# Four graph layers in one kernel: the attention stage's node products at the end of PE's step, and two batches of forward gathers begun behind the scatter

## The chip, the cores and the metric

One NeuronCore of a Trainium2 chip runs the whole program. The metric is the device time of one execution in microseconds, lower is better. The kernel is written directly in instructions for each engine: PE (TensorE, matrix products), DVE (VectorE), ACT (ScalarE), POOL (GpSimd, here the issuer of indirect DMAs) and SP (SyncE, here the issuer of plain DMAs). Engines wait for each other on semaphores only.

## The reference

Four layers run one after the other on a graph of 6250 nodes with 128 features and 106250 edges (two directions of 50000 edges, and a loop on every node), each followed by a residual and a layer norm: `x = layernorm(x + layer(x))`. Edges come sorted by destination. The first layer is attention with 8 heads of 16, and this is what it computes:

```python
q, k, v = (einsum('ni,hid->nhd', x, W) + b for W, b in ((Wq, bq), (Wk, bk), (Wv, bv)))
e = edge_weight[:, None, None] * We[None]
alpha = einsum('ehd,ehd->eh', q[dst], k[src] + e) / sqrt(16)
m = segment_max(alpha, dst)
ex = exp(alpha - m[dst])
w = ex / max(segment_sum(ex, dst)[dst], 1e-16)
agg = segment_sum(w[:, :, None] * (v[src] + e), dst)
out = (agg + skip).reshape(n, 128) @ Wo + bo + x
out = layernorm(out) * gamma + beta
```

The second layer is an edge MLP with a segment sum by destination, the third a filter (`c * (W(edge_attr) * h1[src])`, summed by destination). The fourth is gated: it takes the mean of `x @ W_in` over sources for each destination, and of `x @ W_out` over destinations for each source, and puts both through a GRU cell with `x` as its state.

## The kernel before

The edges lie in 880 tiles of 128 (with fillers, so that no tile crosses more than one bucket of 128 destinations). Four tiles are a batch (U = 4), so each stage runs over BATCHES = 220 batches; the nodes are 49 buckets of 128. For each batch POOL issues four indirect DMAs, one for each tile, which gather the rows of the edges' sources (`gather_rows`, L694) into a ring: six batches deep in the attention stage (KR), seven in the gated one (FR). There are four stages: attention (about 190 to 1415 us), edge MLP (1422 to 2440), filter (2540 to 3650) with a scatter of the rows into an order by source (3650 to 4818, L2221, four indirect DMAs for each batch), and the gated stage (4860 to 6007).

**Attention stage.** Each engine has a loop of its own over slots `s`, and the order of the calls in its body is the order of its work; semaphores tie the loops together. In slot `s` PE multiplies one-hot rows with the queries of batch `s` (`query`, L888), and sums batch `s - 10` into PSUM (`total`, L934: eight products, two of each tile, in two halves; a half waits until DVE has added the half before it to the accumulator, semaphore `added`). DVE multiplies and reduces batch `s - 1` (`products`, `head_sums`), weighs the messages of batch `s - 9` (`weigh`, `message`, L1201) and makes four adds to the accumulator for batch `s - 11` (`add`, L1224), spread over its step. ACT makes the one-hot matrices (`edge_hot`, `turned_hot`) and copies the values out of the gather ring (`keep_values`, L1021), which frees the ring for POOL.

Four batches are a chunk, with its softmax maximum found by scans over the edges. The chunk's work is spread over four phases, `ph = s % 4`, and hops between PE and DVE. In phase 1 PE transposes the scores (`turn_scores`, L896) and DVE scans them in phase 2 (L1157). At the end of phase 2 PE turns the ends of the runs (`turn_runs`, L899 and L900), and DVE walks over them at the start of phase 3 (`walk`, L1169). At the end of phase 3 PE turns the carries (`turn_carries`, L909), ACT copies them in phase 0 (L1039), DVE scans again. At the end of phase 0 PE turns the maximum back (`return_max`, L914, L899, L900), and DVE subtracts it at the start of phase 1 (`shift`, L1188). Before the `total` of each chunk's first batch PE makes `rank_one` (L922, L923). In PE's slot all these transposes stand behind `total`.

**Node parts.** Once all edges of a bucket are added (slot NODE_AT), its 128 nodes go through the rest of the layer in small parts, each in a slot of its own: DVE joins the heads (lag 1), PE turns them (`turn_heads`, lag 2, L944, L945), PE multiplies by Wo (`mix_heads`, lag 3, L949 to L951), DVE's first and second norm (lags 4 and 5) and renewal (lag 6), PE turns the new nodes (`turn_nodes`, lag 7, L955) and projects them for the next layer (`project`, lag 8, L960 to L962). `node_sums(s)` holds PE's parts and `take_nodes(s)` ACT's copies of them out of PSUM (L1063 for the first, L1066, L1068, L1075 and L1076 for the others). DVE's node parts stand last in its slot.

**From the scatter to the gated stage.** A stage's work stands in blocks; all engines meet between two blocks. The filter stage's block ends on POOL with the scatters, then gathers for the first FR = 7 batches of the gated stage into its ring, then a wait for the scatters' landing. In the gated stage's block DVE begins with two memsets of 128 x 6400 elements (L2408, L2409) and then makes the one-hot matrices of the forward part, PE sums batch 0 (`gl_sum_f`, L2376) and so frees the first slot of the ring, for which POOL's next gather waits. SP loads the rows in order by source.

Of the kernel before, what the change touches and what calls it, by code (L numbers as in the profile page):

```python
# [40 lines left out]
KR, FR = 6, 7  # L41
TILES = -(-(E // P + NB) // (U * R)) * U * R
BATCHES = TILES // U
# [726 lines left out]
def node_due(s, lag):  # L770

    return NODE_AT.index(s - lag) if s - lag in NODE_AT else None
# [12 lines left out]
def stage_attention(nc, c, t, small_weights):  # L785


    with ExitStack() as ctx:
# [38 lines left out]
        maxed, returned, shifted, fallen, exped = (sem(n) for n in ("maxed", "returned", "shifted", "fallen", "exped"))  # L827
        ranked, rescaled = sem("ranked"), sem("rescaled")
        hots, exs, ews, messages, summed, added = (sem(n) for n in ("hots", "exs", "ews", "messages", "summed", "added"))
        SLOTS_N = NODE_AT[-1] + PROJECTED + 1  # L830
        PREPARED = 11
        block = ctx.enter_context(nc.Block())

# [7 lines left out]
        @block.sync  # L841
        def _(sp):
            def load_skip(n):
                at = bucket_in_turn(nc, c, n, SP_ENGINE)
                at_least(sp, given, node_groups_before(NODE_AT[n - 2] + TURNED + 1) if n >= 2 else 0, None)
                sp.dma_start(skip[:, n % 2, :], c.skip[bass.ds(at, 1), :, :].rearrange("one p f -> p (one f)")).then_inc(skipped[n % 2], 16)

            def send_rows(n):
                at = bucket_in_turn(nc, c, n, SP_ENGINE)
                sp.wait_ge(taken, node_reads_before(NODE_AT[n] + PROJECTED + 1))  # L850
                sp.dma_start(c.table3[bass.ds(at, 1), :, :].rearrange("one p f -> p (one f)"), rows_out[:, n % 2, :]).then_inc(row_sent[n % 2], 16)

            sp.dma_start(last, c.key[P - 1:P, :]).then_inc(lasts, 16)
            for to, of in small_weights:
                sp.dma_start(to, of).then_inc(weights, 16)
            sp.dma_start(c.table3[NT - 1, :, :], c.x[:, NT - 1, :]).then_inc(padded, 16)
            for k in range(SLOTS_N + 4):
                n = node_due(k, -2)
                if n is not None:
                    load_skip(n)  # L860
                n = node_due(k, PROJECTED + 4)
                if n is not None:
                    send_rows(n)
                if k >= BATCHES:
                    continue
                at_least(sp, hots_t, 2 * (k - R + 1), None)
                load_local_rows(sp, c, rows, k, k % R, rows_in)
                if k % CB == CB - 1:
                    n = k // CB
                    if n == 0:  # L870
                        sp.wait_ge(start, 4)
                    at_least(sp, maxed, 2 * (n - 1), None)
                    breaks = c.breaks[n * CT:(n + 1) * CT, :].unsqueeze(0).broadcast_to([H, CT, P])
                    sp.dma_start(pen[:, n % 2, 0:P], breaks).then_inc(pens_in[n % 2], 16)
            sp.wait_ge(padded, 16)
            for q in range(2):
                sp.wait_ge(row_sent[q], 16 * len(range(q, NB, 2)))

        @block.tensor
        def _(pe):  # L880
# [94 lines left out]

            for s in range(SLOTS_N):
                ph, n = phase(s)
                if s < BATCHES:
                    query(s)
                node_sums(s)  # L980
                km = s - LAG - 1
                if 0 <= km < BATCHES:
                    if km % CB == 0:
                        rank_one(km // CB)
                    total(km)
                if ph == 1 and 0 <= n < CHUNKS:
                    turn_scores(n)
                if ph == 2 and 0 <= n < CHUNKS:
                    turn_runs(n)
                if ph == 3 and 0 <= n < CHUNKS:  # L990
                    turn_carries(n)
                if ph == 0 and 0 <= n - 1 < CHUNKS:
                    return_max(n - 1)

        @block.scalar
        def _(act):
# [81 lines left out]
            for s in range(SLOTS_N):  # L1078
# [2 lines left out]
                    turned_hot(0)  # L1081
                if 0 <= s - LAG - 1 < BATCHES:
                    edge_hot(s - LAG - 1)
                if ph == 0 and 0 <= n - 1 < CHUNKS:
                    carries(n - 1)
                if s + 1 < BATCHES:
                    turned_hot(s + 1)
                for lag, w in ((FIRST, 0), (SECOND, 1)):
                    if node_due(s, lag + 1) is not None:
                        inverse_root(node_due(s, lag + 1), w)  # L1090
                if ph == 1 and 0 <= n - 1 < CHUNKS:
                    exponents(n - 1)
                if 0 <= s - 1 < BATCHES:
                    keep_values(s - 1)
                if 0 <= s - LAG < BATCHES:
                    exps(s - LAG)
                if ph == 1 and 0 <= n < CHUNKS:
                    spreads(n)
                take_nodes(s)

        @block.vector
        def _(dve):
# [202 lines left out]
def stage_edges(nc, c, name, table, acc, buckets, local, layer, h1, ring, arrived, begun, next_rows=None):  # L1305
# [5 lines left out]
    with ExitStack() as ctx:  # L1311
# [60 lines left out]
        def _(pool):  # L1372
            gather_rows(pool, c, table, ring, arrived, [(freed, 1)], range(begun, BATCHES))
            if layer == 2:
                for k in range(BATCHES):
                    c.by_source.scatter(pool, k)
                pool.wait_ge(c.by_source.tabled, 16)
                gather_rows(pool, c, c.table, c.by_source.ring_f, c.by_source.arrived_f, [], range(FR))
                for r in range(R):
                    pool.wait_ge(c.by_source.scattered[r], 16 * U * BATCHES // R)  # L1380
            if layer == 1:
# [590 lines left out]
        stage_attention(nc, c, t, small_weights)  # L1972


E1_R, BEGUN = 6, 3


def stage_src_lists(nc, c, t, loads, before, previous, w_both, b_both, ring, arrived):
# [285 lines left out]
def stage_gated(nc, c, fwd, rev, ring_f, arrived_f, p_in, p_out, gate_rows, out):  # L2264
# [5 lines left out]
    with ExitStack() as ctx:  # L2270
# [16 lines left out]

        @block.gpsimd
        def _(pool):
            gather_rows(pool, c, c.table, ring_f, arrived_f, [(summed_f, 1)], range(FR, BATCHES))  # L2290

        @block.sync
        def _(sp):
# [318 lines left out]
```

## Time and profile before

| | |
|---|---|
| time, median of 3 runs | 6020.16 us (6016.43 to 6023.98) |
| profiled execution, its own time | 6009.66 us |
| its span | 6007.6 us |
| mean granted clock of PE, share of full speed | 0.778 |
| PE busy | 3885.8 us (65% of the span) |
| DVE busy | 3669.8 us (61%) |
| ACT busy | 2801.3 us (47%) |
| POOL busy | 4295.4 us (71%) |
| chain that ended last | POOL 13% of the span, issue 4%, PE 1% |

The shares are means over four stages with different limits, so they say little by themselves. Rows further down come from windows (busy time of each engine in a stretch of the span), from the list of waits (which engine stood at which line, and for whom), and from the timeline (start and length of each instruction in us, and in brackets the idle time before it with what ended it). L934 is line 934 of the kernel. A line may group some instructions of one kind that follow each other: x4 are four of them, and the length is that of all.

### The profile page before, as it was taken

The page shows a single profiled execution, that of the slowest core. Times are in us where ns is not written, and L with a number is a line of the kernel's source. Part 1 is how long each engine was busy: PE and PEld are TensorE (multiplying, and loading weights), DVE is VectorE, ACT ScalarE, POOL GpSimd, SP SyncE. Part 2 cuts the span into 40 slices and gives each one's busy share as a digit, 9 for nine tenths or more (in the row PEclk, how much of TensorE's full clock was granted, in tenths as well). Part 3 has the DMA queues.
Part 4 walks back from the last instruction along what each step waited for, and adds up shares of the span by engine and source line. Part 5 has one row for each costly group of instructions (what it writes and reads, how often), then busy time and mean ns, then how long its engine had stood idle before and what let it go on. Part 6 is the DMA issues. An engine that isn't in the chain of part 4 may idle for free. (4 is left out here: it accounts for less than half of the span.)

```text
span 6007.6 us, 92656 instructions
## 1 busy us (share of the span) xinstructions
PE 3885.8 (65%) x20652; PEld 3141.3 (52%) x20652; DVE 3669.8 (61%) x11763; ACT 2801.3 (47%) x6925; POOL 4295.4 (71%) x4477
## 2 busy tenths in 40 slices
PE   5577777775766776678888887444344346666665
PEld 5466666664555555545655655333333346664443
DVE  6788888886988888666777765111011034445665
ACT  3688888882211111145555654111111158884444
POOL 2677777763777777767777777777777767777775
PEclk8788878887999888878888887555555579898887
DMA  4444444453755555622333325333233245552223
GB/s 125 121 136 131 130 131 129 128 116 101 200 149 145 149 148 148 127 65 74 74 77 74 75 73 100 83 79 78 78 79 78 70 133 168 165 166 79 58 57 45
DMA packets 485359, 652.55 MB, mean 109 GB/s; under 512 B 119512, under 2 KB 332245, under 8 KB 484822
## 3 DMA queue, kind: packets, MB, share of 16 engines
q0 software_dynamic: 155552, 349.05, 23.3%
q1 hardware_dynamic: 329271, 297.58, 18.8%
q8 instruction: 187, 3.06, 0.2%
q14 instruction: 349, 2.86, 0.2%
HBM read 495.44 MB, written 150.71 MB: 108 GB/s over the span
## 5 line engine op out<-in xcount | busy, mean ns | idle before, releaser
L694 POOL DMA_INDIRECT kv_ring<-keys_values,gather_i x880 | 862.2, 980 | 348.9 <-issue 258.4
L694 POOL DMA_INDIRECT arena<-table,gather_i x880 | 856.4, 973 | 291.1 <-issue 266.4
L694 POOL DMA_INDIRECT e_ring<-filter_rows,gather_i x880 | 841.8, 957 | 299.8 <-issue 267.9
L2221 POOL DMA_INDIRECT rows_by_src<-arena,key x880 | 858.3, 975 | 268.7 <-issue 267.6
L694 POOL DMA_INDIRECT e_ring<-table,gather_i x880 | 844.5, 960 | 275.0 <-issue 264.8
L2133 PE MATMUL e_pt<-nodes,arena 128*128 x1728 | 442.5, 437 | 628.5 <-ACT arena L2142 620.9
L2133 PEld LDWEIGHTS e_pt<-nodes,arena 128*128 128x128 f32 x1728 | 381.2, 325 | 690.3 <-issue 690.3
L2125 DVE TENSOR_SCALAR arena<-arena,part 128x512 f32<-128x512 bf16 x220 | 115.2, 525 | 913.1 <-PE e_pt L2133 910.9
L2376 PE MATMUL gl_sum_f<-arena,gl_hot_f 128*128 128x128 f32 x1760 | 282.6, 310 | 446.0 <-DMA arena<-table,gather_i 173.9
L1582 PE MATMUL e_pa<-e_msg,e_hot 128*128 128x128 f32 x3520 | 543.9, 305 | 30.5 <-DVE e_msg L1803 22.7
L743 DVE TENSOR_TENSOR arena<-arena,e_pa 128x128 f32 x1760 | 497.4, 283 | 99.9 <-PE e_pa L1582 70.5
L934 PE MATMUL at_pa<-at_msg,at_hot 128*128 128x145 f32 x1760 | 379.3, 358 | 230.1 <-DVE arena L1224 209.5
L1582 PEld LDWEIGHTS e_pa<-e_msg,e_hot 128*128 128x128 f32 x3520 | 503.4, 220 | 42.9 <-DVE e_msg L1803 34.6
L2376 PEld LDWEIGHTS gl_sum_f<-arena,gl_hot_f 128*128 128x128 f32 x1760 | 243.8, 214 | 485.1 <-DVE gl_hot_f L2416 292.1
L1563 PE MATMUL e_ph<-l_w1e_by_tile,e_attr 128*128 128x512 f32 x440 | 281.5, 726 | 328.5 <-DVE e_tmp L1798 300.7
L2140 ACT ACTIVATE arena<-src_local 128x4 f32<-128x4 bf16 x216 | 45.0, 208 | 932.7 <-DMA rows_by_src<-arena,key 932.5
L934 PEld LDWEIGHTS at_pa<-at_msg,at_hot 128*128 128x128 f32 x1760 | 297.4, 232 | 295.3 <-issue 217.9
L1456 ACT ACTIVATE e_msg<-e_tmp 128x512 f32<-128x512 f32 x220 | 138.6, 630 | 632.8 <-DVE e_tmp L1798 629.2
L1554 PE MATMUL e_pt<-e_attr,L_mlp_w_held 50*128 50x512 f32 x440 | 273.3, 704 | 187.5 <-DVE e_soft L1809 184.8
L2323 ACT ACTIVATE gl_hot_r<-j,arena 128x128 f32<-128x128 f32 x1024 | 324.3, 387 | 150.2 <-PE gl_sum_r L2367 86.9
L888 PE MATMUL at_pq<-arena,at_hot_t 128*128 x1760 | 333.6, 348 | 55.6 <-ACT at_hot_t L1006 44.7
L1565 PEld LDWEIGHTS e_ph<-arena,e_hot_t 128*128 128x128 f32 x1760 | 281.2, 228 | 131.0 <-issue 131.0
(463 smaller groups left out, 9784.5 us busy)
## 6 DMA issues: line engine op xcount, KB each, us to landing
rows_by_src<-e_filler SPq DMA_DIRECT2D x256, 260.0 KB
arena<-rows_by_src SPq DMA_DIRECT2D x256, 260.0 KB, 2.9
at_rows<-local_rows SPq DMA_DIRECT2D x220, 128.0 KB, 3.5
e_rows<-local_rows SPq DMA_DIRECT2D x220, 128.0 KB
arena<-local_rows SPq DMA_DIRECT2D x220, 128.0 KB
e_attr<-edge_attr SPq DMA_DIRECT2D x880, 25.0 KB
kv_ring<-keys_values,gather_i POOLq DMA_INDIRECT x880
e_ring<-table,gather_i POOLq DMA_INDIRECT x880
```

The source lines that it names most:

```text
L694: pool.indirect_dma_start(ring[:, r, u, :], None, table, bass.IndirectOffsetOnAxis(index, 0)).then_inc(arrived[r], 16)
L743: self.dve.tensor_tensor(to, to, self.psum[:, u, 0:self.width], ALU.add).then_inc(self.added, 1)
L888: ins = pe.matmul(pq[:, q, u, 0:QW], hot_t[:, q, u, :], c.query[:, bass.ds(which[u], 1), :].rearrange("p one f -> p (one f)"), start=True, ...
L934: ins = pe.matmul(sum_of(u), hot[:, q, u, :], msg[:, q, u, :], start=True, stop=True)
L1554: pe.matmul(pt[:, r % 2, :, :].rearrange("p u f -> p (u f)"), c.w["mlp_w0"][:, :], attr[:, r, :], start=True, stop=True).then_inc(ready, 1)
L1563: pe.matmul(ph[:, q, :, :].rearrange("p u f -> p (u f)"), attr[:, r, :], c.w["w1e_by_tile"][:, :], start=True, stop=False)
L1565: ins = pe.matmul(ph[:, q, u, :], hot_t[:, r, u, :], c.by_dst[:, bass.ds(which[u], 1), :].rearrange("p one f -> p (one f)"), start=False, ...
L1582: ins = pe.matmul(pa[:, q, u, :], hot[:, r, u, :], msg[:, q, u, :], start=True, stop=True)
L2133: ins = pe.matmul(ph[:, k % 2, u, :], self.hot_t[:, k % R, u, :], self.c.x[:, bass.ds(which[u], 1), :].rearrange("p one f -> p (one f)"), ...
L2221: pool.indirect_dma_start(self.table, bass.IndirectOffsetOnAxis(place, 0), self.out[:, r, u, :], None)\
L2323: act.activation(hot_r[:, r, u, :], c.j[:, 0:P], ACT.Abs, bias=ring_r[:, j % RR, u, F + 1:F + 2], scale=-1.0).then_inc(hots_r, 1)
L2376: ins = pe.matmul(sum_f[:, q, u, :], hot_f[:, r, u, :], ring_f[:, k % FR, u, :], start=True, stop=True)
```

## The change

In the attention stage PE's `node_sums(s)` moves from its place between `query` and `rank_one`/`total` to behind `total`, ahead of the transposes. ACT's `take_nodes` moves from the end of the slot to a place behind `turned_hot` and takes the products of the slot before; `turned_hot` comes ahead of `carries`, and `keep_values` ahead of `exponents`. The stage has one slot more, and SP's sending of node rows stands one slot later. Behind the scatter two batches of forward gathers are begun (BEGUN_F), not seven; the gated stage's block issues the rest.

```diff
-        SLOTS_N = NODE_AT[-1] + PROJECTED + 1
+        SLOTS_N = NODE_AT[-1] + PROJECTED + 2
...
-            for k in range(SLOTS_N + 4):
+            for k in range(SLOTS_N + 5):
...
-                n = node_due(k, PROJECTED + 4)
+                n = node_due(k, PROJECTED + 5)
...
                 if s < BATCHES:
                     query(s)
-                node_sums(s)
                 km = s - LAG - 1
                 if 0 <= km < BATCHES:
                     if km % CB == 0:
                         rank_one(km // CB)
                     total(km)
+                node_sums(s)
                 if ph == 1 and 0 <= n < CHUNKS:
                     turn_scores(n)
...
                     edge_hot(s - LAG - 1)
+                if s + 1 < BATCHES:
+                    turned_hot(s + 1)
                 if ph == 0 and 0 <= n - 1 < CHUNKS:
                     carries(n - 1)
-                if s + 1 < BATCHES:
-                    turned_hot(s + 1)
+                take_nodes(s - 1)
                 for lag, w in ((FIRST, 0), (SECOND, 1)):
                     if node_due(s, lag + 1) is not None:
                         inverse_root(node_due(s, lag + 1), w)
+                if 0 <= s - 1 < BATCHES:
+                    keep_values(s - 1)
                 if ph == 1 and 0 <= n - 1 < CHUNKS:
                     exponents(n - 1)
-                if 0 <= s - 1 < BATCHES:
-                    keep_values(s - 1)
                 if 0 <= s - LAG < BATCHES:
                     exps(s - LAG)
                 if ph == 1 and 0 <= n < CHUNKS:
                     spreads(n)
-                take_nodes(s)
...
-                gather_rows(pool, c, c.table, c.by_source.ring_f, c.by_source.arrived_f, [], range(FR))
+                gather_rows(pool, c, c.table, c.by_source.ring_f, c.by_source.arrived_f, [], range(BEGUN_F))
...
-E1_R, BEGUN = 6, 3
+E1_R, BEGUN, BEGUN_F = 6, 3, 2
...
-            gather_rows(pool, c, c.table, ring_f, arrived_f, [(summed_f, 1)], range(FR, BATCHES))
+            gather_rows(pool, c, c.table, ring_f, arrived_f, [(summed_f, 1)], range(BEGUN_F, BATCHES))
```

## Rows read from the trace of the kernel before

**Rows 1.** windows of the attention stage: busy time of each engine, granted clock
```profile
core 0: us, PE busy (x) PEld busy (x) DVE busy (x) ACT busy (x) POOL busy (x), PEclk, DMA share, GB/s
300.00:1200.00 900.00, 660.22 (x3713) 575.43 (x3710) 779.70 (x2568) 760.20 (x2087) 653.77 (x668) 0.82 0.47 131
710.00:718.00 8.00, 5.26 (x20) 4.55 (x21) 5.70 (x19) 5.30 (x14) 6.17 (x7) 0.50 0.45 119
841.00:847.00 6.00, 5.78 (x44) 5.26 (x45) 5.70 (x18) 5.90 (x18) 3.50 (x4) 1.00 0.26 68
```

**Rows 2.** waits, 300 to 1200 us: us in total, times, longest
```profile
POOL kv_ring L694 <- ACT arena L1021: 49.3, 52, 3.2
PE at_pa L934 <- DVE arena L1224: 159.2, 135, 3.5
...
ACT arena L1066 <- PE at_pn L955: 22.7, 16, 3.2
...
DVE at_ends L1169 <- PE at_p_turn L900: 13.9, 12, 1.6
...
DVE at_alpha L1188 <- PE at_p_turn L900: 7.6, 9, 1.4
...
DVE at_msg L1201 <- ACT at_ex L1045: 5.5, 10, 0.7
```

**Rows 3.** timeline of one step with phase 0 and two node products
```profile
745.56 0.22 PE L949 MATMUL at_pn<-bias_rows,ones_bf 65*128 65x128 bf16 x1
...
746.40 0.44 PE L962 MATMUL at_pn<-l_wk,at_x_t 128*128 128x128 f32 x2
...
747.51 0.76 PE L934 MATMUL at_pa<-at_msg,at_hot 128*128 128x145 f32 x4 [0.17 <-DVE arena L1224]
...
748.67 0.28 DVE L1188 TENSOR_TENSOR at_alpha<-at_alpha,at_p_turn 128x128 f32<-128x128 f32 x1
```

**Rows 4.** timeline, PE's node products of the two other pairs
```profile
817.86 0.22 PE L949 MATMUL at_pn<-bias_rows,ones_bf 65*128 65x128 bf16 x1
...
818.41 0.39 PE L955 MATMUL at_pn<-ident,arena 128*128 128x128 f32 x2
...
838.49 0.38 PE L944 MATMUL at_pn<-ident,arena 128*128 128x128 f32 x2
...
838.94 0.39 PE L955 MATMUL at_pn<-ident,arena 128*128 128x128 f32 x2
```

**Rows 5.** timeline, two steps with phase 2, PE at either clock
```profile
713.49 0.30 DVE L1224 TENSOR_TENSOR arena<-arena,at_pa 128x145 f32 x1
...
717.92 0.28 DVE L1169 COPY at_ends<-at_p_turn 1x128 f32<-1x128 f32 x1 [1.54 <-PE at_p_turn L900]
...
843.85 0.30 DVE L1224 TENSOR_TENSOR arena<-arena,at_pa 128x145 f32 x1
...
846.47 0.28 DVE L1169 COPY at_ends<-at_p_turn 1x128 f32<-1x128 f32 x1
```

**Rows 6.** timeline, last scatters, gathers, start of the gated stage
```profile
4799.49 0.21 ACT L2140 ACTIVATE arena<-src_local 128x4 f32<-128x4 bf16 x1 [4.41 <-DMA rows_by_src<-arena,key]
...
4817.59 0.97 POOL L2221 DMA_INDIRECT rows_by_src<-arena,key  x1 [0.30 <-issue]
...
4861.48 5.39 DVE L2408 MEMSET arena<- 128x6400 f32 x1 [88.94 <-issue]
...
4876.75 0.94 POOL L694 DMA_INDIRECT arena<-table,gather_i  x1 [23.19 <-PE gl_sum_f L2376]
```

**Rows 7.** timeline of POOL and DVE where another stage begins
```profile
1439.74 0.94 POOL L694 DMA_INDIRECT e_ring<-table,gather_i  x1 [3.12 <-POOLq L1980]
...
1440.49 5.39 DVE L1682 MEMSET arena<- 128x6400 f32 x1 [8.72 <-issue]
...
1444.73 0.94 POOL L694 DMA_INDIRECT e_ring<-table,gather_i  x1 [0.30 <-issue]
```

**Rows 8.** the chain that ended last, gated stage
```profile
5909.03 2.59 DMA arena<-table,gather_i
```

## The prediction, made before the change was run

> **What bounds the kernel now.** I read the page first (shares of busy time, the slices), then windows of each stage, then the waits and the timeline of the attention stage, and last the place between the scatter and the gated stage. The change touches two places: the attention stage (about 190 to 1415 us) and the end of the filter stage's block with the start of the gated stage (4818 to 4877 us).
>
> In three of the four stages Pool issues indirect gathers or scatters without a pause: 0.94 us for one and 0.30 us before the next, so 1.25 us each and 5.0 us a batch [rows 6, 7]. The attention stage is the exception. 900 us of it hold Pool's 668 gathers, 167 batches, so 5.4 us a batch. Pool is held 49.3 us there by ScalarE's copy of the values (L1021) [rows 1, 2]. The last of four engines is busiest: VectorE with 779.7 of 900 us, ScalarE 760.2, PE 660.2 [rows 1]. VectorE stands for another engine in only 13.9 + 7.6 + 5.5 = 27.0 us [rows 2]; the rest of its idle time (120.3 - 27.0 = 93 us) is its own (register loads, results that it waits for itself) and some smaller waits. So VectorE sets the step. And what holds it is nearly always PE's transposes: L900 before the walk (L1169) and before the shift (L1188) [rows 2]. Those transposes stand at the end of PE's step, behind the second half of `total`, and that half waits for VectorE's last add of the same step: PE spends 159.2 us on these adds [rows 2]. The reader should see a ring: VectorE's add, PE's half total, PE's transposes, VectorE's next step. Its slack is small: in a step with phase 0 the half total starts at 747.51 with a wait on the add, and the shift is there at 748.67, 1.16 us later [rows 3].
>
> **The change, part by part.**
>
> First, PE's node products move from ahead of `rank_one` and `total` to behind them. The work is the same; only its cover changes. In the old place it lies in time in which PE would wait for VectorE's adds anyway. In [rows 3] the six products run from 745.56 to 746.84 and the second half of `total` still waits at 747.51 for the add; without them the first half would run earlier and the second would start at 747.51 all the same. In the new place they lie between that half and the transposes, where nothing covers them, and each of the ring's steps is late by their length less the slack.
>
> Their length, at full clock: 1.28 us for mixing with projecting [rows 3]; 818.41 + 0.39 - 817.86 = 0.94 us for mixing with turning again; 838.94 + 0.39 - 838.49 = 0.84 us for turning the heads with turning again [rows 4]. Mean 1.02, taken as 1.0 since the end of one overlaps the next instruction by 0.1.
>
> How often: buckets come every 4.49 steps (220 batches over 49 buckets), and a bucket has products at lags 2, 3, 7 and 8. In nine steps that gives three doubled steps (the three pairs above) and two single ones. In the single ones VectorE has a part of its own for a node (renewing, or the first norm) at the end of its step, which covers 0.7 us of products; I cost these at nothing, and if that cover is gone they cost 2 x 24 x 0.4 = 19 us more. Doubled: 220/9 = 24.4 times 3 = 73, or 18 for each of the four phases.
>
> What each phase pays: phase 0 (transposes for the shift) 18 x 1.0 = 18; phase 1 (transposed scores for the scan, some 0.25 us of slack, as VectorE starts its step with products) 18 x 0.75 = 13.5; phase 2 (rows for the walk, behind `rank_one`) 18 x 1.0 = 18; phase 3 (carries, which ScalarE takes with room) nothing. Sum 49.5. In about one of six of these steps PE was already behind the add (steps with the slow clock, as in the first of [rows 5]), so that the old place was exposed too and nothing is added: 49.5 x 5/6 = **+42 us** (41.3). Bounds: nothing, if VectorE finds other work in that time or the drift of the engines absorbs it; +50 if every doubled step pays, +69 with the single ones.
>
> Second, ScalarE takes the node products one step later, in the middle of its step and not at its end, and keeps the values before the exponents. ScalarE waited 22.7 us for PE at L1066, for products just issued; that goes, since the products are then a step old. It makes ScalarE freer, and Pool's 49.3 us behind the values smaller [rows 2]. But neither is on VectorE's way: it waited for ScalarE 5.5 us in 900 [rows 2], 7.5 us over the stage's 1225. I cost this at -3, inside the rounding of the 42, between 0 and -7.5. For VectorE the later copy is still early: the first norm stands last in its step, behind four adds. The exponents come one copy (some 0.5 us) later; `weigh` reads them several steps on.
>
> Third, the slots: one more at the end of the stage (SLOTS_N + 1), SP's rows sent one slot later. After the last batch only node parts run in a slot, and the last products are taken in the next slot instead of the same one. Below 2 us; costed at nothing.
>
> Fourth, the gathers for the gated stage begun behind the scatter: two batches, not seven. 5 x 4 = 20 gathers, 20 x 1.25 = 25 us, go from the filter stage's block to the gated block. That block begins once Pool is through, so all of it begins 25 us earlier. Before, Pool issued 28 gathers from 4817.59 + 0.97 + 0.30 = 4818.86 to 4853.56 and then stood for 23.19 us, until PE's first forward sum was done at 4876.75 [rows 6]. After: the eight gathers end at 4818.86 + 10.0 - 0.3 = 4828.6; entering the next block takes Pool 3.12 us where another stage begins [rows 7], and at most 7.9 here (from 4853.56 to VectorE's first instruction there, 4861.48); I take 7.2, nearer to the row of this place. Then 25 us of gathers, so the batch that needs a freed slot is issued at 4828.6 + 7.2 + 25.0 = 4860.8, where it was 4876.75. PE's first sum is done by 4876.75 - 25 = 4851.7 and holds nobody. Gain **-16 us** with 7.2 us, -15 with 7.9, -20 with 3.1. Is the end of the scatter then uncovered, with only 8 gathers behind it? The packing at 4799.49 was released by a batch of scatters 1.4 us after its last issue; 10 us of gathers cover that. And the gain reaches the end: the chain that ended last still runs over Pool's gathers up to 5909.03 [rows 8].
>
> A rule of the Trainium skill speaks against this last gain. Row first: where the edge stage begins, a gather took 0.94 us at 1444.73 beside a memset of 5.39 us on VectorE [rows 7], no longer than without one. The skill (GPSIMD Engine Reference, section 1, Specifications) says that GpSimd shares its SBUF interfaces with VectorE and contends with VectorE instructions in a two-port mode. By that rule the 20 gathers would stand for the two memsets, 10.8 us, and the gain would be 5, not 16; the row does not show it.
>
> Sum: +42 - 16 = +26 us. The profiled execution took 6009.66 us; with 26 more, 6035.7. The median shown is 6020.16, 10.5 us above that execution, so the predicted time is **6046 us**.
>
> **Rivals.** 0.2% of this kernel is 12 us, about what its measurement can tell from no change; the cases below are sorted by that.
>
> A. The attention stage doesn't change, since VectorE takes up the delay: the waits it shows are only 27 of 900 us [rows 2], and one could read that as room. Then only the gated part is left: 6020 - 16 = 6004, faster. For it: 93 us of VectorE's idle time have no other engine behind them, and a delay could coincide with them. Against it: they are spread in pieces over its step, and the order on each engine is fixed. 0.15.
>
> B. The exposure is there but a third of the size (a doubled step with 0.6 us of slack), and it cancels the gain: +14 - 16 or so, 6010 to 6030, no change. 0.17.
>
> C. ScalarE's relief pays. If the waits of VectorE go away, since ScalarE is never late and the sums come early, 27.0 x 1225/900 = 37 us go from the stage at most; with the 16 that is 6020 - 35 - 16 = about 5970. It decides if ScalarE is what makes PE late in the ring (PE waits for its one-hot rows, too). For it: ScalarE is busy 760 of 900 us. Against: 0.07, for PE's wait ends with VectorE's add, not with ScalarE.
>
> D. The clock. At the granted clock of 0.50 (1.2 GHz) the way from VectorE's second add to the walk took 717.92 - 713.49 - 0.30 = 4.1 us; at 1.00 (2.4 GHz) 846.47 - 843.85 - 0.30 = 2.3 us [rows 1, 5]. The change takes products out of the wait ahead of `rank_one`, so PE is idle in longer pieces there. If one of six phase 2 steps more falls to the lower clock, 9 x 1.8 = 16 us are added, and with other phases some 25: about 6070, 6058 to 6090. The skill (TensorE: Matmul & The Clock Gate, What's actually happening) puts it so that the throttled state is the default and activity releases it; by that rule longer gaps cost clock, and the two rows agree in the levels. 0.12.
>
> **How the numbers follow.** The forecast has 0.49: 6032 to 6058, from +28 to +54 in the stage against 16 (with the gated gain of only 5 inside it). D 0.12, slower too. B 0.17, same. A 0.15 and C 0.07, faster. So faster 0.22, same 0.17, slower 0.61. The range runs from 5995 (it holds A, not C) to 6080 (it holds most of D): about 0.9 of the cases, of which I count 0.8 for the sizes being off.
>
> **What would show it.** In the trace of the changed kernel: in the attention stage L900 as releaser of L1188 and L1169 with two to three times the waits, some 50 to 70 us in 300 to 1200, and the stage (first batch to the edge stage) longer by 42; in steps with products the order L934, L944 to L962, L914/L899/L900, with the shift later by the products' length. ScalarE's waits at L1066 and L1063 near nothing; Pool's waits for L1021 down. At the gated start: 8 gathers, then VectorE's memset 25 us earlier, no wait of 23 us on L2376, the freed batch's gather 16 us earlier. Wrong it would be if the waits at L1169 and L1188 do not grow: then the old place was not covered, or the slack is larger than I read. It would also be wrong if ScalarE's waits turn up at Pool or VectorE elsewhere, or if the gathers beside the memsets take more than 1.25 us apart.

## The result and the profile after

The changed kernel takes 6079.78 us (median of 4 runs, 6065.05 to 6089.54), the kernel before 6018.3 us beside it; the ratio is 1.0093, with a 95% interval of 1.0082 to 1.0105. That is 56 us more (49 to 63). The prediction was 6046, 26 more: the right direction, and less than half of the size. All microseconds given for experiments below are such ratios times 6018.

First the windows of the attention stage of the changed kernel, which answer to [rows 1]:

```profile
core 0: us, PE busy (x) PEld busy (x) DVE busy (x) ACT busy (x) POOL busy (x), PEclk, DMA share, GB/s
300.00:1200.00 900.00, 639.38 (x3461) 562.28 (x3461) 732.12 (x2399) 709.29 (x1946) 612.44 (x627) 0.78 0.45 122
906.00:912.20 6.20, 5.99 (x25) 5.48 (x26) 2.61 (x9) 3.05 (x8) 3.30 (x4) 0.50 0.43 126
```

In the same 900 us the engines do less work: Pool issues 627 gathers, not 668, VectorE is busy 732 us, not 780. The granted clock of PE is 0.78, not 0.82, and there are stretches of 0.50 in which PE is busy nearly all the time (5.99 of 6.20 us). Next who waits for whom, in total, times and longest, beside [rows 2]:

```profile
POOL kv_ring L694 <- ACT arena L1021: 96.6, 75, 3.4
...
ACT at_carry L1039 <- PE at_p_turn L909: 80.9, 38, 5.1
...
DVE at_ends L1169 <- PE at_p_turn L900: 40.3, 18, 3.4
...
ACT arena L1063 <- PE at_pn L945: 31.4, 9, 4.0
...
DVE at_alpha L1188 <- PE at_p_turn L900: 18.3, 16, 2.0
...
DVE at_run L1157 <- PE at_p_turn L896: 10.9, 16, 1.5
...
DVE at_run L1181 <- ACT at_carry L1039: 10.4, 14, 1.4
```

VectorE's wait at the walk (L1169) went from 13.9 to 40.3 us, at the shift (L1188) from 7.6 to 18.3. Two waits are new: 10.9 us for the transposed scores (L1157) and 10.4 us for ScalarE's copy of the carries (L1181). ScalarE waits no less for products than before (31.4 + 26.4 us at L1063 and 9.3 at L1066, 67 in all, where it was 55): taken in the next slot they would be old if ScalarE were behind PE, but it runs ahead. Pool's wait for the values did not go down but doubled, from 49.3 to 96.6 us. Both were said otherwise in the prediction.

From the first query to the edge stage's memset the profiled executions, one of each kernel, give 1349.4 us after and 1268.4 before, 81 us more. The pair of [rows 3], again 1.28 us long, in the new place (a slot of phase 1): the transpose of the scores comes behind it.

```profile
832.24 0.22 PE L949 MATMUL at_pn<-bias_rows,ones_bf 65*128 65x128 bf16 x1
...
833.08 0.44 PE L962 MATMUL at_pn<-l_wk,at_x_t 128*128 128x128 f32 x2
...
833.35 0.27 PE L896 MATMUL at_p_turn<-ident,at_alpha 128*128 128x128 f32 x1
```

A step of phase 2 with two node products, PE at the lower clock throughout (the second window above); it answers to [rows 5]:

```profile
906.73 0.30 DVE L1224 TENSOR_TENSOR arena<-arena,at_pa 128x145 f32 x1
...
907.44 2.30 PE L934 MATMUL at_pa<-at_msg,at_hot 128*128 128x145 f32 x8
...
909.54 0.31 PE L949 MATMUL at_pn<-bias_rows,ones_bf 65*128 65x128 bf16 x1
...
910.61 0.63 PE L955 MATMUL at_pn<-ident,arena 128*128 128x128 f32 x2
...
911.25 0.42 PE L900 MATMUL at_p_turn<-ident,at_top 128*1 128x128 f32 x1
...
911.70 0.28 DVE L1169 COPY at_ends<-at_p_turn 1x128 f32<-1x128 f32 x1 [3.35 <-PE at_p_turn L900]
```

The last add ends at 907.03 and the walk begins at 911.70: the rows show the whole way between VectorE's add and VectorE's wait. `total` takes 2.10 us to the first product (1.10 in x9 below, at the higher clock), the products 910.61 + 0.63 - 909.54 = 1.70 (0.94 in [rows 4]), and VectorE stands 3.35 us.

Last the start of the gated stage, beside [rows 6]:

```profile
4907.89 0.97 POOL L2221 DMA_INDIRECT rows_by_src<-arena,key  x1 [0.30 <-issue]
...
4917.95 0.95 POOL L694 DMA_INDIRECT arena<-table,gather_i  x1 [0.30 <-issue]
...
4924.43 0.94 POOL L694 DMA_INDIRECT arena<-table,gather_i  x1 [5.54 <-POOLq L1311]
4925.18 5.39 DVE L2408 MEMSET arena<- 128x6400 f32 x1 [62.32 <-issue]
...
4949.77 0.94 POOL L694 DMA_INDIRECT arena<-table,gather_i  x1 [0.30 <-issue]
```

Eight gathers, 5.54 us to enter the block in place of the wait of 23.19 us, the memset 17.3 us behind the last scatter (43.9 before), and the freed batch's gather 41.9 us behind it (59.2 before): 17.3 us earlier.

### The profile page after: what moved, and what is told of

Its sections match the earlier page's. It is cut to its first block and busy times, and to the rows that moved or that the text cites. A ratio compares the mean times of both kernels' runs of the same rounds, so it can differ in the third digit from the quotient of the medians.

```text
span 6087.5 us, 92656 instructions
## 1 busy us (share of the span) xinstructions
PE 3904.8 (64%) x20652; PEld 3166.2 (52%) x20652; DVE 3671.2 (60%) x11763; ACT 2803.0 (46%) x6925; POOL 4304.8 (71%) x4477
## 5 line engine op out<-in xcount | busy, mean ns | idle before, releaser
L934 PE MATMUL at_pa<-at_msg,at_hot 128*128 128x145 f32 x1760 | 395.0, 370 | 272.6 <-DVE arena L1224 261.3
L1582 PEld LDWEIGHTS e_pa<-e_msg,e_hot 128*128 128x128 f32 x3520 | 499.9, 219 | 43.9 <-DVE e_msg L1803 40.1
L934 PEld LDWEIGHTS at_pa<-at_msg,at_hot 128*128 128x128 f32 x1760 | 312.2, 242 | 342.0 <-issue 279.8
```

The lines of the kernel that those rows point to most:

```text
L934: ins = pe.matmul(sum_of(u), hot[:, q, u, :], msg[:, q, u, :], start=True, stop=True)
L1582: ins = pe.matmul(pa[:, q, u, :], hot[:, r, u, :], msg[:, q, u, :], start=True, stop=True)
```

## The experiments

**One part at a time.** x1 has the kernel before with BEGUN_F = 2:

```diff
-                gather_rows(pool, c, c.table, c.by_source.ring_f, c.by_source.arrived_f, [], range(FR))
+                gather_rows(pool, c, c.table, c.by_source.ring_f, c.by_source.arrived_f, [], range(BEGUN_F))
...
-            gather_rows(pool, c, c.table, ring_f, arrived_f, [(summed_f, 1)], range(FR, BATCHES))
+            gather_rows(pool, c, c.table, ring_f, arrived_f, [(summed_f, 1)], range(BEGUN_F, BATCHES))
```

> Only the second part of the change: two forward batches begun behind the scatter, the attention stage as before. Theory (Pool's idle time before the freed batch shrinks, the rest of the gated stage follows): 16 us less, at most 18; the wait of 23 us for PE's first sum is gone and 3 to 6 us of entering the block stand in its place. Rival 1 (given back inside the gated stage, which ran from the freed batch's gather to its end 7 us longer in the changed kernel): 10 us less. Rival 2 (gathers held by VectorE's two memsets): 5 us less, with gathers over 1.25 us apart in the first 11 us.

Measured 6008.77 us, ratio 0.9976 (0.9967 to 0.9985): 14 us less (9 to 20). Pool's waits around the start:

```profile
POOL arena L694 <- POOLq L1311: 5.5, 1, 5.5
...
POOL arena L694 <- PE gl_sum_f L2376: 0.3, 1, 0.3
```

The 23 us are gone, and 5.5 us stand in their place. 16 us lie inside the interval, the 5 us of the memset rival don't. The 10 us of Rival 1 lie inside it too, so the time alone doesn't rule it out. From the freed batch's gather to the end, though, the profiled executions of the four kernels with two batches begun (the changed one, x1, x4, x10) took 1129 to 1141 us (mean 1135) and those of the ten with seven 1128 to 1137 (mean 1133): they overlap, and no giving back of 7 us shows. x2 is the other part alone (BEGUN_F = 7 in the changed kernel):

> Only the first part: the attention stage as changed, seven forward batches begun behind the scatter as before. Theory (both parts add up, and the attention part is larger than forecast: single products and the carries' phase pay too, phase 2 pays more than the products' length): 65 to 80 us more than before. The forecast's term was 42 more. Rival (the parts are not additive: the edge stage's 8 us more come from the attention stage's new order of arrival): the edge stage longer by 8 us here as well, where chance alone would leave it at 1142 us.

6096.27 us, 1.0124 (1.0109 to 1.014): 75 us more (66 to 84). The parts add up: 75 - 14 = 61, against 56 measured with both. The edge stage took 1144.1 us here and 1150.9 in x1, where nothing ahead of it was changed, so its 8 us in the changed kernel's profile are no effect of the change.

**PE's move and ScalarE's order apart.** x3 moves `node_sums` behind `total` and leaves ScalarE as it was. x5 keeps PE as it was and changes ScalarE's order (with the extra slot, and with the values kept ahead of the exponents, not shown here):

```diff
--- x3, against the kernel before
-                node_sums(s)
                 km = s - LAG - 1
...
                     total(km)
+                node_sums(s)
```

```diff
--- x5, against the kernel before (PE unchanged)
+                if s + 1 < BATCHES:
+                    turned_hot(s + 1)
                 if ph == 0 and 0 <= n - 1 < CHUNKS:
                     carries(n - 1)
-                if s + 1 < BATCHES:
-                    turned_hot(s + 1)
+                take_nodes(s - 1)
...
-                take_nodes(s)
```

> Only PE's move: node products behind total, ScalarE's order, the slots and everything else as before. Theory (the place of PE's products is the whole cost): the same 65 to 80 us more as with all of the attention part. Rival (ScalarE, which takes the products at the end of the same slot, now waits for them behind total, and starts its one-hot matrices of the next slot late, so that PE is late in turn): clearly more, 90 to 130 us, with ScalarE's waits for the products above 100 us; then the reorder on ScalarE is what makes PE's move bearable.

> ScalarE's new order alone, with the extra slot: the node products are taken in the next slot, values kept ahead of the exponents; PE's products in their old place, seven forward batches begun. Theory (VectorE sets the step and hardly waits for ScalarE, 5.5 us of 900): within 10 us of before. Rival (ScalarE's relief pays, since ScalarE no longer waits for products at the end of its slot): 10 to 35 us less. It is also the kernel against which the next three are read.

x3: 6238.58 us, 1.0362 (1.0348 to 1.0376), 218 us more, above even the rival's 90 to 130. Its waits:

```profile
POOL kv_ring L694 <- ACT arena L1021: 202.2, 87, 5.5
...
ACT arena L1063 <- PE at_pn L945: 82.8, 15, 6.8
...
ACT arena L1063 <- PE at_pn L955: 76.9, 16, 5.9
...
DVE at_run L1181 <- ACT at_carry L1039: 48.9, 19, 3.9
...
DVE at_msg L1201 <- ACT at_ex L1045: 29.5, 20, 1.9
```

ScalarE waits 160 us at L1063 alone for products at the end of PE's slot, and then starts its next slot late. VectorE pays at the carries (48.9) and at the messages (29.5; 5.5 in [rows 2]), Pool at the values (202.2; 49.3 before). x5: 6015.07 us, 1.0001 (0.9992 to 1.001), no change, as the theory had it. In its list of waits ScalarE no longer stands for a node product at all, and Pool's wait for the values is 45.7 us: the relief comes, and nothing is gained by it. So ScalarE's order gives nothing by itself and takes two thirds of the price off PE's move: 75 us in place of 218.

**Behind the transposes.** x4 is the changed kernel with PE's products last in the slot:

```diff
                     total(km)
-                node_sums(s)
...
                     return_max(n - 1)
+                node_sums(s)
```

> The changed kernel, but PE's node products stand behind the transposes, last in its slot, not ahead of them. Theory (what costs is that the products stand between VectorE's last add and the transposes for which VectorE waits): VectorE's waits at the walk, the shift and the scan fall back to those of before, the attention stage takes 1268 us or less, the whole 6000 to 6010. Rival 1 (lower clock from longer gaps ahead of rank_one): the gaps stay, so a good part of the loss stays, 6030 to 6060. Rival 2 (products delay the next slot's query and with it VectorE's products): 6030 to 6060 as well, but with VectorE waiting for the query.

6013.54 us, 0.9984 (0.9975 to 0.9993), 10 us less than before (4 to 15); with x1's 14 taken out, some 5 us remain of 75, which is within the noise of the two intervals. VectorE's waits for the transposes:

```profile
DVE at_ends L1169 <- PE at_p_turn L900: 17.2, 13, 2.4
...
DVE at_alpha L1188 <- PE at_p_turn L900: 9.8, 17, 0.8
```

They stood at 40.3 and 18.3 in the changed kernel, at 13.9 and 7.6 before; the wait for the scores (L1157) is gone. The attention stage of this execution took 1283.8 us, not the 1268 or less of the theory (before 1268.4, x1 1273.9). The same work at the same end of PE's slot, but behind the transposes, costs little: what costs is that it lies on the way from VectorE's add to VectorE's wait.

**By slots.** The next five have the attention part with a condition: in the slots named, the products stand behind `total`, in all others in the old place (x7: `ph in (2,)`; x8, x11, x12: phases 3, 0, 1; x6: slots in which only one bucket has products). x7, against the kernel before (ScalarE's part is not shown):

```diff
                     query(s)
-                node_sums(s)
+                if ph not in (2,):
+                    node_sums(s)
...
                     total(km)
+                if ph in (2,):
+                    node_sums(s)
```

> The attention part of the change, but only the slots with a single bucket's products have them behind total; the doubled ones keep the old place. The forecast's step: nothing, since VectorE's own node part covers them. Theory after the table of steps (a slot that turns the heads makes VectorE's next step 0.3 to 0.9 us longer, a slot that projects makes it 0.0 to 0.1 longer): 18 us more than with ScalarE's order alone.

> The attention part, but only in slots of phase 2 (whose transposes the walk waits for) do the products stand behind total. The forecast's step: 18 steps at 1.0 us, less a sixth, 15 us. Theory (these steps are also those with rank_one and the lower clock, and pay more than the products' length at full clock): 30 to 35 us more than with ScalarE's order alone.

> The attention part, but only in slots of phase 3 (whose transposed carries ScalarE copies for VectorE's next scan) do the products stand behind total. The forecast's step: nothing, ScalarE takes them with room. Theory after the table of steps (VectorE's scan then waits for the carry): 15 us more than with ScalarE's order alone.

> The attention part, but only in slots of phase 0 (whose transposed maximum VectorE subtracts in the next step) do the products stand behind total. The forecast's step: 15 us (18 steps at 1.0 us, less a sixth). Theory after the table of steps: 14 us more than before.

> The attention part, but only in slots of phase 1 (whose transposed scores VectorE scans in the next step) do the products stand behind total. The forecast's step: 11 us (18 steps at 0.75 us, less a sixth). Theory after the table of steps: 16 to 20 us more than before, single products that turn the heads included.

| slots with late products | ratio (95% interval) | us more | forecast's term |
|---|---|---|---|
| x6, single ones | 1.0031 (1.002 to 1.0042) | 19 | 0 |
| x11, phase 0 | 1.003 (1.0019 to 1.0041) | 18 | 15 |
| x12, phase 1 | 1.0022 (1.0014 to 1.0031) | 13 | 11 |
| x7, phase 2 | 1.0049 (1.0035 to 1.0062) | 29 | 15 |
| x8, phase 3 | 1.0042 (1.0028 to 1.0056) | 25 | 0 |

x6 and x11 came out near their theories, x7 at the edge of its 30 to 35, x12 below its 16 to 20 and x8 well above its 15. The four phases (single ones are in them) add to 85 us, a little over the 75 of all at once, and each interval is 5 to 8 us wide on either side. In x8's waits VectorE stands for the carry copied by ScalarE (its L1184 is L1181 of the kernel before):

```profile
DVE at_run L1184 <- ACT at_carry L1042: 11.6, 17, 1.4
```

Where in the step each microsecond goes is seen by the length of VectorE's steps. The table is worked out from the timelines: a step runs from one first product of VectorE (L1137) to the next, VectorE's slots 30 to 215, one profiled execution each; rows are by the phase of the PE slot before it and by what node products that slot has (T: turning the heads alone; P: projecting alone; two: any of the three pairs). x1, whose attention stage is that of the kernel before, gives the noise: 5.45 where before has 5.56 in the doubled slots of phase 0, 6.51 where it has 6.32 in those of phase 2, 1019.8 in the sum. Mean us of a step:

```
slot of products     before    x5    x4    x2    x9   changed
phase 0 none   x20     5.26  5.26  5.27  5.26  5.26  5.26
phase 0 T      x5      4.37  4.25  4.50  5.20  5.35  5.30
phase 0 P      x6      5.54  5.53  5.66  5.54  5.53  5.53
phase 0 two    x15     5.56  4.98  5.74  5.98  5.77  6.04
phase 1 none   x22     5.47  5.47  5.45  5.45  5.44  5.45
phase 1 T      x5      4.24  4.28  4.27  5.14  5.07  5.13
phase 1 P      x5      5.74  5.74  5.75  5.74  5.74  5.74
phase 1 two    x15     4.95  4.97  4.95  5.81  5.56  5.72
phase 2 none   x21     6.32  6.34  6.31  6.31  6.34  6.31
phase 2 T      x6      6.65  6.65  6.68  7.49  7.48  7.44
phase 2 P      x5      6.54  6.53  6.52  6.54  6.53  6.53
phase 2 two    x15     6.32  6.87  6.46  7.72  6.98  7.96
phase 3 none   x20     5.28  5.29  5.29  5.29  5.29  5.29
phase 3 T      x5      3.90  3.91  3.96  4.27  4.27  4.26
phase 3 P      x5      5.57  5.62  5.67  5.69  5.72  5.70
phase 3 two    x16     4.76  4.75  4.85  5.38  4.79  5.53
sum, all 186 steps   1017.6 1017.4 1026.1 1083.2 1056.6 1089.0
```

Steps without products are the same to 0.03 us in every kernel. Slots that only project are covered, as forecast (0.1 us more in phase 3); slots that only turn the heads are not, 0.8 to 0.9 us each in three phases and 0.4 in phase 3. A slot of phase 1 that turns the heads, first in the kernel before:

```profile
662.04 0.46 PE L944 MATMUL at_pn<-ident,arena 128*128 128x128 f32 x2 [0.64 <-issue]
662.34 0.39 PE L945 MATMUL at_pn<-ident,arena 128*128 128x128 f32 x2
...
666.96 0.42 PE L896 MATMUL at_p_turn<-ident,at_alpha 128*128 128x128 f32 x1
```

and in the changed kernel:

```profile
693.68 0.63 PE L944 MATMUL at_pn<-ident,arena 128*128 128x128 f32 x2
694.11 0.64 PE L945 MATMUL at_pn<-ident,arena 128*128 128x128 f32 x2
694.53 0.42 PE L896 MATMUL at_p_turn<-ident,at_alpha 128*128 128x128 f32 x1
...
694.99 0.42 DVE L1157 TENSOR_TENSOR_SCAN at_run<-at_pen,at_p_turn 128x128 f32<-128x128 f32 x1 [0.92 <-PE at_p_turn L896]
```

The transpose takes 0.42 us in both, against 0.27 at full clock (the row at 833.35 above): PE is at the lower clock at this place in either kernel. In the old place the products came before that and took 662.34 + 0.39 - 662.04 = 0.69 us; in the new one they run at the lower clock too and take 694.11 + 0.64 - 693.68 = 1.07. So it is in all 21 slots of this kind in the table, in the changed kernel, in x2 and in x9.

**The clock.** x9 is x2 with work put back where the products had stood: in slots with two node products PE issues its four query products twice, the second time with the same values into the same sums.

```diff
-                for u in range(U):
+                for u in list(range(U)) * (2 if sum(node_due(k, lag) is not None for lag in NODE_READS) == 2 else 1):
                     ins = pe.matmul(pq[:, q, u, 0:QW], hot_t[:, q, u, :],
```

> The attention part of the change with PE's query products of a slot issued twice in the slots with two node products (the second time into the same sums, with the same values), that is, work put where the node products stood before; seven forward batches begun. It adds 73 x 4 products to PE. Theory (about half of the excess in phases 2 and 3 is PE's lower clock, which comes in the half of these slots after the gap that the products left): some 20 us less than the 75 us of the attention part alone, so 50 to 60 more than before, and the share of these slots with the lower clock falls back to that of before. Rival (the clock has no part, the place of the products is all): 75 us more, or over it if the added products delay total.

6064.39 us, 1.0081 (1.0068 to 1.0094): 49 us more than before, so 26 less than x2 (14 to 38 by the two intervals), for 264 added products: of the 71 slots with two node products, 66 still have queries. The windows of x9, and its counterpart of the step of phase 2 shown above:

```profile
300.00:1200.00 900.00, 654.15 (x4011) 581.67 (x4010) 754.71 (x2476) 734.54 (x2012) 628.52 (x645) 0.84 0.45 126
888.00:896.00 8.00, 6.19 (x45) 5.63 (x44) 6.50 (x20) 6.82 (x20) 4.89 (x6) 0.94 0.46 130
```

```profile
890.53 0.31 DVE L1224 TENSOR_TENSOR arena<-arena,at_pa 128x145 f32 x1
...
891.00 1.26 PE L934 MATMUL at_pa<-at_msg,at_hot 128*128 128x145 f32 x8
...
892.10 0.22 PE L949 MATMUL at_pn<-bias_rows,ones_bf 65*128 65x128 bf16 x1
...
892.65 0.39 PE L955 MATMUL at_pn<-ident,arena 128*128 128x128 f32 x2
...
893.30 0.28 DVE L1169 COPY at_ends<-at_p_turn 1x128 f32<-1x128 f32 x1 [1.14 <-PE at_p_turn L900]
```

The clock is 0.84 over the 900 us and 0.94 around this step. The last add ends at 890.84 and the walk begins at 893.30, 2.5 us where the changed kernel took 911.70 - 907.03 = 4.7. Take a stretch to be at the lower clock when the clock granted over it is below 0.75 in the mean. In the table's 61 slots with two products:

| at the lower clock | before | x4 | x2 | changed | x9 |
|---|---|---|---|---|---|
| second half of `total` | 4 | 14 | 18 | 23 | 0 |
| the node products | 12 | 13 | 23 | 25 | 0 |

x4 shows that the lower clock alone costs little: it comes more often there too, but only `total` lies on VectorE's way, the products behind it don't. The table of steps says where x9 helps: phase 2 by 0.74 us a step, phase 3 by 0.59 (back to 4.79, no loss at all), phase 1 by 0.25, phase 0 by 0.21. That it is the clock, and not something else that the added products do, is seen inside x2: steps of one phase with one pair of products, by the clock that the products had (mean us of a step; the pairs are mixing and projecting, mixing and turning again, turning the heads and turning again):

| phase, pair | x2, full clock | x2, lower clock | x9, full clock |
|---|---|---|---|
| 0, turning and turning | 4.74 (2 steps) | 5.98 (3) | 4.62 (5) |
| 1, turning and turning | 4.49 (2) | 5.82 (3) | 4.52 (5) |
| 2, turning and turning | none | 7.43 (5) | 5.76 (5) |
| 2, mixing and turning | 7.19 (4) | 9.62 (1) | 7.65 (5) |
| 2, mixing and projecting | 7.62 (3) | 8.67 (2) | 7.54 (5) |
| 3, turning and turning | 3.88 (2) | 4.55 (3) | 3.88 (5) |
| 3, mixing and turning | 5.13 (4) | 6.02 (2) | 5.13 (6) |
| 3, mixing and projecting | 5.28 (1) | 6.72 (4) | 5.28 (5) |

The other pairs of phases 0 and 1 were at full clock in all their steps. Steps at full clock are mostly as long in x2 as in x9, and the 23 at the lower clock are 30 us longer in sum than x9's of the same kind. x9 won 27 of them in these steps; the rest it lost again where the added products made a step longer (7.65 against 7.19).

x10 tried the same with the kernel before, in the 107 slots that have queries and no node products, and with BEGUN_F = 2:

```diff
+                for u in list(range(U)) * (2 if not any(node_due(k, lag) is not None for lag in NODE_READS) else 1):
```

> The kernel before with two forward batches begun, and PE's query products issued twice in the slots that have no node products. It adds about 100 x 4 products to PE. Theory (in 35 to 50 in 100 of these slots total runs at the lower clock, and VectorE's waits for the transposes, 27 us in 900, lie there): 15 us less from the gathers and 0 to 20 more from the attention stage, 5983 to 6003 where before is 6018. Rival (the second products delay what VectorE waits for in its own slot): slower than with two batches begun alone.

6011.84 us, 0.9989 (0.9981 to 0.9998): 7 us less than before (1 to 11), where two batches begun alone gave 14 (9 to 20). It missed its theory's 15 to 35 us less; the rival had the result, slower than two batches begun alone, though the two intervals touch. The window of 300 to 1200:

```profile
300.00:1200.00 900.00, 683.30 (x4225) 607.35 (x4225) 769.20 (x2532) 750.62 (x2056) 642.01 (x659) 0.86 0.46 129
```

The clock is higher than in any other kernel here, 0.86, and the attention stage is no shorter for it: the steps without products stay at 5.26, 5.46, 6.30 and 5.28 us, and by the table's count the 186 steps take 1030.7 us, 11 more than in x1. Nearly all of that lies in the five slots of phase 0 that mix and project: 7.56 us a step against 5.63 in x1, with the products at the lower clock in four of the five and in none of x1's. So the rival's reason (a delay in the slot itself) is not what the steps show. The fastest version measured is x1, the kernel before with two batches begun; x4's interval overlaps with its own.

## Why the prediction was right in its direction and short in its size

The direction came from the right mechanism. What failed are terms of the sum: the clock, which I left out of it, and two kinds of slots that I put at nothing.

*What bounds the stage, and the way from add to transposes.* Shown. Steps without products don't move in any kernel of the table, and the same products behind the transposes (x4) cost some 5 us where ahead of them they cost 75.

*The doubled slots, +42.* The mechanism holds, the sizes in part by luck. I counted 73 such slots, 18 in each phase; 66 of them have a batch to sum behind them, 16, 15, 17 and 18 by phase. Over before the table gives 0.42 x 15 + 0.86 x 15 + 1.40 x 15 + 0.62 x 16 = 50 us for x2, times 66/61 for the slots outside the table: 54. With the clock held up (x9) it gives 0.21, 0.61, 0.66 and 0.03 us in phases 0 to 3, by the same sum 25 us. So at full clock 42 was too much, and the clock that I left out made up for that and more. The 15 + 11 for phases 0 and 1 look well met by the 18 + 13 of x11 and x12, but some 4 and 6 us of these belong to slots that only turn the heads. The sixth that I took off, for slots already at the lower clock, was too much as well: it was 4 of 61, and the slow step of [rows 5] that I read it from belongs to a slot that only turns the heads.

*The first step that failed: the clock outside the sum.* I priced the products at full clock and put the clock down as rival D with 0.12, "some 25" us. It is no alternative to the forecast but comes with it: x9 measures 26 us (75 - 49), and the steps at the lower clock in x2 are 30 us longer than their like. The products leave a gap in PE's work ahead of `rank_one` and `total`, the granted clock in those slots is lower more often, and then `total`, the products and the transposes, all on VectorE's way, are longer. This is much of why phase 2 cost 29 and not 15. It is also why phase 3 ("carries, which ScalarE takes with room") cost 25 and not nothing: ScalarE does take the carries with room, as long as PE runs at full clock (4.79 us in x9 against 4.76 before), and not at the lower one (4.55, 6.02 and 6.72 us in x2 where the full clock has 3.88, 5.13 and 5.28). By the rule of the Trainium skill that I cited (TensorE: Matmul & The Clock Gate, What's actually happening), throttled is the default and activity releases it. x9, faster by 26 us with 264 products more, agrees.

*The second: "I cost these at nothing, and if that cover is gone they cost 2 x 24 x 0.4 = 19 us".* They cost 19 (x6, 12 to 25), the same figure by luck: not 48 slots at 0.4 us, but the 24 that turn the heads at 0.4 to 0.9 us, and the others nearly nothing. VectorE's node part in a slot that projects is the first norm, in a slot that turns the heads it is only the renewal. Groups of VectorE's instructions (busy time and mean ns), changed kernel:

```profile
L1263 DVE TENSOR_SCALAR arena<-arena,at_mean,at_root 128x128 f32<-128x128 f32 x34 | 11.7, 345 | 0.0
...
L1244 DVE TENSOR_TENSOR arena<-nodes,l_beta 128x128 f32<-128x128 f32 x34 | 9.8, 288 | 0.0
...
L1246 DVE BATCH_NORM_STATS2 at_stat<-arena 128x6 f32<-128x128 f32 x34 | 9.7, 285 | 0.0
...
L1248 DVE BATCH_NORM_AGGREGATE at_mean<-at_stat 128x2 f32<-128x6 f32 x34 | 6.2, 182 | 1.2
```

The first norm's three take 288 + 285 + 182 = 755 ns, as long as the projections' 0.72 us: no loss in the table. The renewal takes 345 ns, and the products that it should cover take 1.06 us, as all of them run at the lower clock in the new place. That leaves 0.7 us of the loss of 0.8 to 0.9; the rest is not accounted for. I had taken one cover of 0.7 us for both, without a row for either, and the products at full clock. x9 adds nothing to these slots, so its 26 us hold none of this.

*ScalarE's order, -3.* Nothing to be measured (x5, 5 us less to 6 more); the -3 is too small to tell. Not foreseen: it is what keeps PE's move from costing 218 us. The table shows two opposite effects in x5 (phase 0 doubled 0.6 us shorter, phase 2 doubled 0.6 longer); with one execution each I don't read more from it.

*The gated part, -16.* 14 measured (9 to 20), and the freed batch's gather 17.3 us earlier. Entering the block took 5.54 us, between the 3.12 and the 7.9 that I had as bounds. The rival by the Trainium skill (GPSIMD Engine Reference, section 1, Specifications), gathers held up beside VectorE's memsets, is out: by it the gain would be 5, below x1's interval, and the ten gathers that Pool issued beside the two memsets took 0.94 or 0.95 us each.

*The sum.* The 41 for the doubled slots became 54 and the single slots' nothing 19, together 73 where x2 measures 75 (66 to 84). With the gated part's -14 that is 59, against 56 measured (49 to 63).

Rivals A (0.15), B (0.17) and C (0.07) are out by x2, which shows the attention part alone 66 to 84 us slower.

What stays open: why filling the empty slots (x10) brings the lower clock into doubled slots of phase 0; why x5's two opposite shifts appear; and how much of the loss in phases 0 and 1 at full clock is slack that I misread. x2 and the changed kernel, the same in this stage, differ little in the products at the lower clock (23 and 25 slots); their timed runs differ by what BEGUN_F explains.

## What to carry to other kernels

In a ring of two engines, ask of each piece of work not how busy its engine is but whether it lies between the partner's last result and the transposes that the partner waits for; there it costs its length less the slack (here 0 to 0.7 us of 1.0 at full clock, and on average 1.3 us more in a step at the lower clock), and a place behind them cost next to nothing here. Work in such a wait has a second use on PE: taken out, it can take the clock down with it, so price a move of PE work at both clocks and in the sum. Where a cover is claimed for several kinds of slots, each kind needs its own row.

## What the hardware showed that was not expected

The kernel got 26 us of 75 back for doing 264 products more on PE (x9), with the clock at 0.84 where x2 has 0.78. The same trick in the slots without products gained nothing: clock 0.86, and no shorter steps (x10). Between the end of Pool's issues in one block and its first gather in the next 5.54 us pass (x1, x4, x10 and the changed kernel alike), against 2.9 to 3.1 us at the start of the edge stage.
